# K and Q turned through memory and VectorE, projection products spread over the scores

## What is computed

```python
q = rmsnorm((x @ Wq).reshape(B, T, 16, 128), q_rms_w)
k = rmsnorm((x @ Wk).reshape(B, T, 16, 128), k_rms_w)
v = (x @ Wv).reshape(B, T, 16, 128)
scores = einsum('bthd,bshd->bhts', q, k) / sqrt(128) - slope[h] * (t - s)   # causal
y = rmsnorm(einsum('bhts,bshd->bhtd', softmax(scores), v), subln_w)
x = layernorm(x + y.reshape(B, T, 2048) @ Wproj)
```

## Time and profile before

| what | value |
|---|---|
| median of 3 runs | 1440.74 us (1440.17 to 1444.86) |
| the profiled execution, run time | 1442.51 us |
| its span, first to last instruction | 1440.7 us |
| TensorE busy | 1400.9 us (97%) |
| VectorE, ScalarE, GpSimd busy | 813.3, 730.3, 424.2 us |
| attention loop | from 21.09 us to about 960 us |
| mean granted TensorE clock | 0.992 of full speed |

### The profile page before, as it was taken

How to read it: one execution, slowest core, us unless ns; L and a number is a source line. 1 busy time by engine, 2 the same in 40 slices (tenths; PEclk the granted TensorE clock), 3 DMA queues, 4 the chain that set the end, 5 groups by cost and what they waited for, 6 DMA issues and landing times. The chain is left out here.

```text
span 1440.7 us, 26432 instructions
## 1 busy us (share of the span) xinstructions
PE 1400.9 (97%) x7744; PEld 1184.6 (82%) x7745; DVE 813.3 (56%) x1877; ACT 730.3 (51%) x1633; POOL 424.2 (29%) x410
## 2 busy tenths in 40 slices
PE   8999999999999999999999999999999989999994
PEld 6888888888888888888888888878887868888783
DVE  6555655656556555555565555567777763333334
ACT  5565656656556566566565565543333223333334
POOL 1212221212112122222121212103445553353565
PEclk9999999999999999999999999999999999999997
DMA  5243333232433333333334245557659546756699
GB/s 185 75 130 95 109 95 115 88 113 91 131 95 109 95 96 108 96 107 109 117 89 115 76 128 157 143 136 171 148 137 233 176 139 247 265 201 230 187 192 237
DMA packets 136851, 200.45 MB, mean 139 GB/s; under 512 B 16624, under 2 KB 83312, under 8 KB 133488
## 3 DMA queue, kind: packets, MB, share of 16 engines
q1 hardware_dynamic: 126032, 149.67, 36.0%
q0 software_dynamic: 10784, 50.36, 11.9%
HBM read 160.05 MB, written 92.62 MB: 175 GB/s over the span
## 5 line engine op out<-in xcount | busy, mean ns | idle before, releaser
L413 POOL TENSOR_TENSOR small<-small,half 128x4 f32<-128x4 f32 x193 | 195.0, 1010 | 764.2 <-DVE small L443 764.2
L557 DVE CUSTOM_DVE_ANT_0 logit<-score_ps,bias 128x128 f32<-128x128 f32 (+3 forms) x256 | 124.8, 487 | 157.1 <-PE score_ps L699 117.6
L347 ACT ACTIVATE prob<-logit,small 128x128 f32<-128x128 f32 (+3 forms) x256 | 144.2, 563 | 120.1 <-DVE small L557 116.5
L712 PEld LDWEIGHTS y_ps<-vs,prob_t 128*128 128x128 f32 x1280 | 175.1, 191 | 21.5 <-ACT prob_t L354 4.5
L712 PE MATMUL y_ps<-vs,prob_t 128*128 (+1 forms) x1280 | 185.6, 276 | 0.7 <-ACT prob_t L354 0.7
L354 ACT ACTIVATE prob_t<-prob_ps 128x128 f32<-128x128 f32 (+3 forms) x256 | 111.5, 436 | 54.9 <-PE prob_ps L705 53.9
L705 PE MATMUL prob_ps<-ident,prob 128*128 128x128 f32 x640 | 112.8, 274 | 3.2 <-ACT prob L347 2.8
L443 DVE TENSOR_REDUCE small<-squares 128x4 f32<-128x516 f32 x128 | 88.4, 691 | 45.7 <-ACT squares L269 43.8
L631 PE MATMUL v_ps<-w_hi,x_hi 128*128 (+1 forms) x256 | 106.7, 417 | 1.4 <-DVE w_lo L488 1.4
L929 ACT ACTIVATE yt_hi<-x_raw,subln 128x512 fp32r<-128x512 f32 x60 | 43.2, 723 | 126.2 <-DVE x_raw L1025 51.2
L631 PE MATMUL v_ps<-w_hi,x_lo 128*128 (+1 forms) x256 | 106.6, 416 | 0.0
(11 more groups left out here) (233 smaller groups left out, 3370.0 us busy)
## 6 DMA issues: line engine op xcount, KB each, us to landing
slots_x<-in_zeros SPq DMA_DIRECT2D x64, 512.0 KB, 4.4
y_scratch<-x_now SPq DMA_DIRECT2D x65, 256.0 KB, 2.8
x_raw<-in_x_t SPq DMA_DIRECT2D x64, 256.0 KB, 2.6
slots_y<-in_zeros SPq DMA_DIRECT2D x64, 256.0 KB, 4.4
y_raw<-y_scratch SPq DMA_DIRECT2D x56, 256.0 KB
w_raw<-in_w_experts POOLq DMA_DIRECT2D x7, 2048.0 KB
w_hi<-in_w_experts POOLq DMA_DIRECT2D x7, 2048.0 KB
w_raw<-in_w_all SPq DMA_DIRECT2D x16, 768.0 KB, 6.1
```

Source lines behind the costliest of these rows:

```text
L347: nc.scalar.activation(prob[:, 0:width], logit[:, 0:width], ACT.Exp, scale=-1.0, bias=least[:, h:h + 1], accum_out=row_sum[:, (i % 2) * HG ...
L413: nc.gpsimd.tensor_tensor(r, ms, half[:, :], ALU.pow).then_inc(ready, 1)
L557: nc.vector.tensor_tensor_reduce(out=logit[:, 0:width], in0=score_ps[:, 0:width], in1=bias[:, h, T - width:T], scale=1.0, scalar=3e38, op0 ...
L712: mm = nc.tensor.matmul(y_ps[:, :].rearrange("p (b h i) -> p h b i", b=QB, h=HG)[:, h, :, :], prob_t[:, j * P:(j + 1) * P], one(vs[:, bass ...
```

## The change

1. K and Q are no longer transposed by TensorE in the loop (only for the first tile, ahead of it). VectorE writes both normalised (`normalise_part`) into one buffer `kq` of 128x1024; SyncE stores it to DRAM (`store_kq`, one DMA of 512 KB) and loads it again with the 32x32 blocks in exchanged places (`load_kq`, four DMAs of 128 KB in runs of 1 KB) into `kq_in`; VectorE transposes within the blocks (`turn_part`, two STREAM_TRANSPOSE of 128x512), into blocks of `w_raw` that have become free. `kt_hi`, `kt_lo`, `qt_hi`, `qt_lo` are then made from SBUF, not from PSUM.
2. To make room for that path in time, projections run two tiles ahead, not one. The 36 products of the second tile move ahead of the loop, and the last two steps have none.
3. The products of a step stand as 12 (K), 6 and 6 (Q), 9 and 3 (V).
4. The buffer of the squares is one for K, Q and y, and so each square waits for the sum before it (`summed`).
5. VectorE and ScalarE lists are in a new order: `split_x` and `normalise` of Q stand at the end of VectorE's step; the weight rounding stands at the start of ScalarE's step, for i = 0 and 1 ahead of `softmax(0)`; `keep_v` stands behind the square of y.
6. The weight load is issued in step i = 3, behind the load of x. Output projection of tile 0 is spread over the last two steps (12+12, 12+12).

```diff
+            def store_kq(t):
+                sp.wait_ge(k_normed, t + 1)
+                sp.wait_ge(q_normed, t + 1)
...
+                    sp.wait_ge(kq_loaded, (t - 1) * (16 * QB))
+                sp.dma_start(kq_scratch, kq[:, :]).then_inc(kq_stored, 16)
+            def load_kq(t):
+                sp.wait_ge(kq_stored, t * 16)
...
+                rows = kq_scratch.rearrange("(a j) (b c) -> b j a c", a=QB, b=QB)
+                for b in range(QB):
+                    sp.dma_start(kq_in[b * QP:(b + 1) * QP, :].rearrange("p (a c) -> p a c", a=QB), rows[b])\
+                        .then_inc(kq_loaded, 16)
...
+            def turn_part(m, out, t, ready, done):
+                dve.wait_ge(kq_loaded, t * (16 * QB))
+                dve.wait_ge(ready, t)
+                nc.vector.transpose(turned_columns(out), in_parts[:, m]).then_inc(done, 1)
...
                     logits(0)
-                    row_means(ysq, y_ms, y_squared, n + 1, y_summed)
+                    row_means(y_sq, y_ms, y_squared, n + 1, y_summed)
...
                     normalise_y(yn[:, i % 2, :], n + 1)
-                    if ahead:
-                        row_means(ksq, k_ms, k_squared, n + 2, k_summed)
                     logits(1)
-                    if ahead:
-                        normalise(kn[:, :], k_ps, k_r, k_rstd, n + 2, k_normed)
...
+                    if projects:
+                        row_means(kq_sq, k_ms, k_squared, n + 3, k_summed)
+                    if i in (1, 2):
+                        split_w(i - 1)
...
+                    logits(2)
+                    if i == 2:
+                        split_w(2)
+                    if ahead:
+                        turn_part(1, kt, n + 1, k_ready, k_turned)
+                        turn_part(0, qt, n + 1, q_ready, q_turned)
+                    if projects:
+                        normalise_part(1, k_ps, k_r, k_rstd, n + 3, k_normed)
...
                     logits(3)
+                    if projects:
+                        row_means(kq_sq, q_ms, q_squared, n + 3, q_summed)
+                    if ahead:
+                        if nxt_i == 0:
+                            keep_first_k(n + 2, kt)
+                        split_k(nxt, nxt_i, n + 2, kt)
+                        split_q(nxt_i, n + 2, qt)
+                    if not (last and i >= 1):
+                        split_x((i + 1) % 2, n + 4)
+                    if projects:
+                        normalise_part(0, q_ps, q_r, q_rstd, n + 3, q_normed)
...
                     score(2)
-                    if ahead:
-                        pe.wait_ge(k_normed, n + 2)
-                        if i == 0:
-                            pe.wait_ge(k_ready, n + 1)
-                        turn(kt_ps, kn, k_turned)
-                        project(v_ps, 2, xb, wp, 0, 4)
+                    if projects:
+                        project(q_ps, 0, xb, wp, 6, 12).then_inc(q_projected, 1)
```

More of the change, by code:

```diff
@@ L224, in body @@
                 for i in range(TB):
-                    if last:
+                    if last and i == TB - 1:
+                        sp.wait_ge(k_ready, its * TB)
+                        sp.wait_ge(q_ready, its * TB)
+                        load_blocks(sp, w_raw[:, CT:2 * CT, :], y_scratch, 0, early_loaded, NHG - 1, NHG)
+                        sp.dma_start(w_raw[:, last_block[i], :], w_last[:, i, :]).then_inc(wp_loaded, 16)
+                    else:
+                        load_kq(it * TB + i + 1)
@@ L242, in body @@
                             .then_inc(x_loaded[i % 2], 16)
+                    if not last and i == TB - 1:
+                        load_w(it + 1)
                     sp.wait_ge(y_normed, it * TB + i + 1)
@@ L251, in body @@
                         .then_inc(y_cleared, 16)
+                    if not (last and i >= TB - 2):
+                        store_kq(it * TB + i + 2)
             with sp.Fori(0, last_it) as it:
@@ L342, in body @@
                     nxt, nxt_i = (it % 2, i + 1) if i < TB - 1 else ((it + 1) % 2, 0)
+                    far, far_i = (it % 2, i + 2) if i < TB - 2 else ((it + 1) % 2, i + 2 - TB)
                     ahead = not (last and i == TB - 1)
+                    projects = not (last and i >= TB - 2)
                     def softmax(h):
@@ L395, in body @@
                     keep_prob_t(3)
[L396 to L398 removed]
+                    if not ahead:
                         round_last(3)
@@ L577, in body @@
-                    if not (last and i >= 2):
-                        split_x(i % 2, n + 3)
-                    if ahead:
-                        row_means(qsq, q_ms, q_squared, n + 2, q_summed)
-                    logits(2)
-                    if ahead:
-                        normalise(qn[:, :], q_ps, q_r, q_rstd, n + 2, q_normed)
-                    else:
-                        split_y(2)
+                    if last and i == TB - 2:
+                        dve.wait_ge(early_loaded, 16 + 32 * QB)
+                        turn_y(2)
@@ L1807, in build @@
         x_raw = sb("x_raw", [P, 2, CT * P])
[L1808 to L1818 removed]
+        kq = sb("kq", [P, 2 * GW])
+        kq_in = sb("kq_in", [P, 2 * GW])
+        x_nat = (kq[:, 0:C], kq[:, C:2 * C])
+        widths = (P, SLOT_TILES * E, CT * E, E, E, E * NT, SLOT_TILES * E)
+        starts = [sum(widths[:j]) for j in range(len(widths))]
+        before, tiles, w_r, experts, run, floors, past = (kq_in[:, s:s + w] for s, w in zip(starts, widths))
+        w_r = w_r.rearrange("p (c e) -> p c e", c=CT)
+        past = past.rearrange("p (k e) -> p k e", e=E)
         const_loaded = sem("p_const_loaded")
```

323 lines of the change are left out of this document (185 added, 138 removed).

## The result

The changed kernel takes 1455.7 us (median of four runs, 1455.0 to 1456.3) against 1441.8 us for the kernel before in the runs beside it: a ratio of 1.0094, interval 1.0075 to 1.0113. It is 0.9% slower, where the forecast said 1403 us and faster. The span of the profiled execution went from 1440.7 to 1453.7 us.

A forecast was written before the change was run, and what follows sets the result against it. TensorE, busy 97% of the span, bounds the kernel. Loop -41, narrow steps of the last iteration -0.9, first load +2.5, last steps +1.1: -38 us on 1440.7, median 1403 us, range 1384 to 1440.

The forecast's parts named there:

- What goes: Eight TensorE transposes of K and Q, 0.88 us a step; if nothing else limits, iterations fall to 54.3 us, gaining 57.
- R: Round trip through DRAM, from the end of normalise Q to the first block transpose: 7.65 us, ends 6.5 and 9.2.
- the loop: One round trip a step, length R + T: binds narrow steps (i = 0, 1), while TensorE binds wide ones (i = 2, 3).
- T: VectorE's path from first block transpose to the end of the next normalise Q: 5.4 to 5.9 us by step.
- 2R + 40.0: Iteration time: narrow steps (i = 0, 1) 2R + 9.1, wide ones 14.4 and 16.5 us; 55.3 us against 58.07.
- rival 1: Round trip hidden if R is under 7.1, so TensorE binds the narrow steps too: 1387 us; chance 0.19.
- rival 4: Skill page's rule: transpose 128x128 on TensorE, VectorE only for blocks of 32, so the change loses; no separate chance given.
- In later iterations the load is issued some 9 us before it is needed, and costs nothing: Weight load with projections two tiles ahead: no cost after the first iteration; without that cover up to 6 us an iteration.
- if wide steps wait too (R too small here): Sign that the forecast is wrong: waits in steps i = 2 and 3, forecast at 14.4 and 16.5 us without them.
- 6 and 6, 9 and 3: nothing: New shares of Q and V products cover the exponentials at no cost; without them some 0.3 us a step.
- The first load: First weight load in the loop, queued behind the first store of K and Q, delays TensorE: +2.5 us once.
- DMA volume: ... nothing: 1 MB more DMA traffic a step on top of 1.3 MB costs nothing, as the fills have landed before the store.

The follow-up runs named there:

- the repaired change: The changed kernel with Q's weights split sooner, first weight load and left-over zero fill issued sooner, and last y summed sooner; 1392.2 us, 0.9658 of the kernel before.
- the longer trip: The kernel with the fill moved, with the K and Q buffer stored twice, first to memory that nothing reads; 1440.4 us, ratio 0.9998.
- the kernel with the fill moved: The changed kernel with Q's weights split sooner, first weight load ahead of first store, and left-over 2304 KB zero fill issued before the loop; 1396.6 us, 0.9697.

## Why the prediction was wrong

**What goes: nearly right.** The ceiling was 54.3 us an iteration (11.0, 12.4, 14.4, 16.5); with all waits out it is 54.9 (10.7, 12.5, 14.9, 16.8). The 0.6 is 9 us over the 15 full iterations. The transposes did leave TensorE, and its busy time is 47 us lower in the repaired change (1400.9 to 1353.6), for the forecast's 55. The saving of 0.88 a step was not met evenly: against the earlier trace rows it is 1.5 us in step 0 and 0.7, 0.4 and 0.6 in the others.

**R and the loop: right, with luck in the terms.** R was 7.3 for 7.65; the store lands in 2.6, below the 3.4 taken, and the load in 2.9, above the 2.3, so two errors partly cancel (the 3.2 and 2.3 that the forecast gave beside its own terms miss in the same way). T was 5.5 us in step i = 1 (522.13 to 527.60), for 5.7. With the longer trip the narrow steps follow the loop, and the whole 2R + 40.0 comes out within 0.3 us, though by errors that cancel. Of the two it was rival 1, the hidden trip, that held for the narrow steps. The rule of the Trainium skill that rival 4 named ("VectorE: DVE Perf Modes", "Rules for kernel authors") is not borne out in this kernel: TensorE is busy for 97% of the span here, and with VectorE and the trip in its place the repaired change as a whole is faster (0.9658); with the longer trip of 8.6 us, the gain of the kernel with the fill moved is gone (0.9998).

**The failed step: "In later iterations the load is issued some 9 us before it is needed, and costs nothing".** It looked at the load and not at what the weights go through next. Being two tiles ahead moved the deadline of the next weights one step forward. The low part of Q's weights then stood behind logits(1), and TensorE's only cover behind score(1) was what waited for it. The forecast's list of who waits for whom followed K, Q and x through VectorE, but not the weights, although the diff shows `split_w(i - 1)` behind logits(1), and in its full length the wait on the weights moved from step i = 3 to i = 2. Its price was 31 us of wait and 12 us of clock, more than the gain of 41. The forecast had no term for the clock at all. One of its signs of being wrong, "if wide steps wait too (R too small here)", did come, but R was not the reason.

**"6 and 6, 9 and 3: nothing": the term stands, the reason does not.** The time of each edit was summed against the kernel as it would be with all of them, and there it is zero: TensorE waits nowhere in the narrow steps. But the forecast looked only at the exponential behind score(1) and put its cover at some 0.3 us a step, 19 us over 64 steps; taken away, the shares cost 34 us, 1.1 and 0.9 in the two narrow steps and next to nothing in the wide ones. What they do beyond covering exponentials is to bring score(2) forward, behind which the new block transposes stand.

**The single terms.** The first load was put at +2.5; moving it won 8.8, of which 5.7 in the step that waited for it. "DMA volume: ... nothing" held in the loop, but not for the one fill of 2304 KB ahead of the last iteration (5.6). The handover to the next part was not looked at (3.6). The last steps, forecast at +1.1, were not measured alone.

With the wait on Q's weights and the first load mended, the time is 1402.3 us, near the forecast's 1403. That is partly chance: narrow steps came out shorter than forecast (10.7 and 12.5 for 11.2 and 13.2) and wide ones longer, and the late fill and handover stood in it.

## What to carry to other kernels

When work is made to run further ahead, every input of it gets an earlier deadline: list them all, with each operation between the load and its use, and look whether any stands in a queue behind the very instruction that the waiting engine has just done. Cost an edit both with the others in place and with it alone removed; one that costs nothing may be what the others rest on. And in an in-order DMA queue look at the single large transfers outside the loop, not only at those in it.

## What was not expected of the hardware

The same idle stretch of TensorE, 2.06 us, took the granted clock down in every second iteration only, and the clock stayed at 1.00 during the stretch itself. Windows of 2 us around the wait in two iterations, columns as above:

```profile
472.60:474.60 2.00, 0.00 (x0) 0.00 (x0) 1.77 (x4) 0.87 (x3) 0.61 (x1) 1.00 0.80 225
474.60:476.60 2.00, 1.94 (x5) 1.57 (x6) 0.00 (x0) 0.00 (x0) 0.78 (x1) 0.55 1.03 266
...
531.40:533.40 2.00, 0.00 (x0) 0.00 (x0) 1.77 (x4) 0.83 (x3) 0.64 (x1) 1.00 0.78 232
533.40:535.40 2.00, 1.98 (x11) 1.71 (x12) 0.00 (x0) 0.00 (x0) 0.74 (x1) 1.00 1.03 279
```

A stretch of 2.7 us took it down in 6 of iterations 1 to 14, one of 0.4 us in none. What decides between two iterations that are alike up to the wait is not shown by any run. Two stores of 512 KB issued 0.39 us apart landed 2.6 and 3.6 us after their issues, so the second delays the trip by 1.3 to 1.4 us and not by a full 2.6.
